# A decoder layer on one core: the search for an expert's threshold, two bits a round instead of one

## What is computed

```python
logits = xf @ router_w + router_b          # 4096 tokens x 8 experts
scores = softmax(logits, axis=-1)
G, idx = top_k(scores.T, 512)              # each expert takes its 512 best tokens
toks = xf[idx]
h1 = relu(toks @ w1 + b1)
eo = h1 @ w2 + b2
y = zeros_like(xf).at[idx].add(eo * G[..., None])
```

## Time and profile before

| | us |
|---|---|
| median of 3 runs | 1249.55 |
| lowest, highest run | 1247.36, 1250.38 |
| the profiled execution | 1243.2 |
| its span | 1241.5 |
| of it the 30 rounds, 972.87 to 1009.74 | 36.87 |
| TensorE busy in the span | 1125.6 |
| VectorE busy in the span | 971.6 |
| ScalarE busy in the span | 711.8 |

### The profile page before, as it was taken

How to read it: one execution, slowest core, us unless ns; L and a number is a source line. 1 busy time by engine, 2 the same in 40 slices (tenths; PEclk the granted TensorE clock), 3 DMA queues, 4 the chain that set the end, 5 groups by cost and what they waited for, 6 DMA issues and landing times. The chain is left out here.

```text
span 1241.5 us, 21939 instructions
## 1 busy us (share of the span) xinstructions
PE 1125.6 (91%) x7644; PEld 668.3 (54%) x7647; DVE 971.6 (78%) x2640; ACT 711.8 (57%) x1429; POOL 584.9 (47%) x676
## 2 busy tenths in 40 slices
PE   4599999999999999999999999999998229999997
PEld 2355555555555555444455454544334117988896
DVE  7688888888889789888888898988872677666653
ACT  6035555555455656777767777776674104566553
POOL 5666586765868563535353535350221004354524
PEclk9779999999999999999999999999999558999999
DMA  5551542525426345252525252424101604544413
GB/s 176 119 119 30 128 95 78 120 57 116 107 83 146 95 107 127 77 109 80 121 69 121 69 120 69 103 71 101 35 18 52 192 0 157 134 112 111 112 27 34
DMA packets 89328, 117.91 MB, mean 95 GB/s; under 512 B 12065, under 2 KB 59105, under 8 KB 89090
## 3 DMA queue, kind: packets, MB, share of 16 engines
q1 hardware_dynamic: 83074, 107.97, 33.9%
q0 software_dynamic: 6144, 8.52, 4.2%
HBM read 48.63 MB, written 16.91 MB: 53 GB/s over the span
## 5 line engine op out<-in xcount | busy, mean ns | idle before, releaser
L823 ACT ACTIVATE probs<-ps_st 128x512 f32<-128x512 f32 (+3 forms) x1024 | 476.6, 518 | 249.8 <-PE ps_st L647 245.4
L667 PE MATMUL ps_p<-kst,qst 63*128 63x512 f32 (+3 forms) x1024 | 371.4, 428 | 14.9 <-DVE mx L940 13.5
L938 DVE TENSOR_REDUCE mx<-ps_p 128x1 f32<-128x512 f32 x512 | 325.4, 681 | 58.6 <-PE ps_p L667 57.8
L647 PE MATMUL ps_st<-qst,kst 64*128 64x512 f32 (+3 forms) x1024 | 362.5, 420 | 9.5 <-ACT probs L823 8.5
L647 PEld LDWEIGHTS ps_st<-qst,kst 64*128 64x128 f32 x1024 | 166.3, 186 | 264.1 <-ACT probs L823 216.4
L940 DVE CUSTOM_DVE_ANT_0 ps_p<-ps_p,tri 128x128 f32<-128x128 f32 (+3 forms) x512 | 239.3, 513 | 16.4 <-PE ps_p L667 14.6
L628 PE MATMUL ps_o<-probs,vals 128*32 128x512 f32 (+3 forms) x2048 | 232.7, 527 | 0.0
L667 PEld LDWEIGHTS ps_p<-kst,qst 63*128 63x128 f32 x1024 | 169.1, 186 | 29.1 <-DVE mx L940 21.5
L468 POOL TENSOR_SCALAR lnw<-mv 128x4 f32<-128x4 f32 x24 | 5.0, 210 | 282.9 <-DVE mv L917 282.8
L533 POOL TENSOR_SCALAR_AFFINE_SELECT probs<-probs 128x512 f32<-128x512 f32 x128 | 79.6, 637 | 102.5 <-ACT probs L823 102.5
L1251 POOL DMA_INDIRECT out_dram<-moe_part,moe_ids x32 | 58.7, 1835 | 75.4 <-DVE moe_part L1614 69.0
(11 more groups left out here) (237 smaller groups left out, 1928.5 us busy)
## 6 DMA issues: line engine op xcount, KB each, us to landing
qst<-qk_h SPq DMA_DIRECT2D x64, 256.0 KB, 4.7
kst<-qk_h SPq DMA_DIRECT2D x64, 256.0 KB, 5.0
qst<-qk_l SPq DMA_DIRECT2D x32, 256.0 KB, 5.4
kst<-qk_l SPq DMA_DIRECT2D x32, 256.0 KB, 5.1
moe_w1r<-in_w_dram SPq DMA_DIRECT2D x8, 1024.0 KB, 5.1
moe_w2r<-in_w_dram SPq DMA_DIRECT2D x8, 1024.0 KB, 9.1
xin<-in_x_dram SPq DMA_DIRECT2D x8, 512.0 KB, 3.8
xres<-in_x_dram SPq DMA_DIRECT2D x8, 512.0 KB, 4.0
```

What stands on the lines that cost most here:

```text
L647: last = nc.tensor.matmul(out, kst[rows, t % 2, pair, kt * P:(kt + 1) * P], qst[rows, t % 2, pair, lo:S], start=True, stop=not masked)
L667: last = nc.tensor.matmul(ps_p1[:, i % 3, 0:keys], qst[rows, t % 2, pair, qt * P:(qt + 1) * P], kst[rows, t % 2, pair, 0:keys], start=True ...
L823: nc.scalar.activation(probs[:, kt, j, 0:n], ps_st[:, i % 2, 0:n], ACT.Exp, scale=float(DH) ** -0.5).then_inc(exp_done, 1)
L938: nc.vector.tensor_reduce(mx[:, g % 2, at:at + 1], bank, AX.X, ALU.max).then_inc(max_done, 1)
```

## The change

Each round now settles two bits and tries three candidates. VectorE counts the scores against two of them (`cand` columns 2 and 3) by two instructions, and ScalarE counts them against the third (column 1) by the function Sign of candidate minus score, summed. TensorE turns the sum of signs into a count by two accumulating products (`same` with a constant column, `same_half` with the signs), and sums the two counts by a third product with two columns. The number of candidates that are met, 0 to 3, is the value of the two bits: VectorE compares three sums with 512 and accumulates (`met`, `won`), and one instruction makes all the next candidates.

The candidates are kept as floats that hold integers, so the 30 bits are searched in two parts: the scores' patterns shifted right by 14 as floats (`high`) in 8 rounds, then the low 14 bits (put into `score`, with the difference of the high parts times 4^7 added) in 7 rounds. The candidates lie half below an integer, so that no sign is zero. In ScalarE's stream the 15 counts stand ahead of `high_w` of expert 0; VectorE waits for GpSimd's `consts` ahead of the search.

```diff
-        BITS = 30
+        HIGH, LOW, HALF = 8, 7, 0.5
...
-            for k in range(BITS):
+            pe.wait_ge(same_ready, 1)
+            for k in range(HIGH + LOW):
+                if k > 0:
+                    pe.wait_ge(cand_ready, k + 1)
+                nc.tensor.matmul(ps_h[:, 0, 0:1], same[:, :], half_all[:, :], start=True, stop=False)
+                pe.wait_ge(cnt_signs, k + 1)
+                nc.tensor.matmul(ps_h[:, 0, 0:1], same_half[:, :], cnt_sign[:, :], start=False, stop=True)
                 pe.wait_ge(cnt_ready, k + 1)
-                nc.tensor.matmul(ps_h[:, 0, 0:1], same[:, :], cnt[:, :], start=True, stop=True).then_inc(cnt_sum, 1)
+                nc.tensor.matmul(ps_h[:, 0, 1:3], same[:, :], cnt[:, :], start=True, stop=True).then_inc(cnt_sum, 1)
...
+            for k in range(HIGH + LOW):
+                act.wait_ge(cand_ready, k + 1)
+                    nc.scalar.activation(sign[:, :, :], high[:, :, :] if k < HIGH else score[:, :, :], ACT.Sign, bias=cand[:, 1:2], scale=-1.0,
+                                         accum_out=cnt_sign[:, :]).then_inc(cnt_signs, 1)
...
-            nc.vector.tensor_copy(same[:, :].rearrange("p (t e) -> p t e", e=E_N), own_row[:, :].unsqueeze(1).to_broadcast([P, P // E_N, E_N]))
+            link(nc.vector.tensor_copy(same[:, :].rearrange("p (t e) -> p t e", e=E_N), own_row[:, :].unsqueeze(1).to_broadcast([P, P // E_N, E_N])))
+            nc.vector.memset(half_all[:, :], float(NT * P // 2 // (P // E_N)))
+            nc.vector.tensor_scalar(out=same_half[:, :], in0=same[:, :], scalar1=-HALF, scalar2=None, op0=ALU.mult).then_inc(same_ready, 1)
...
-            nc.vector.memset(cand[:, :], 1 << (BITS - 1))
+            dve.wait_ge(consts, 1)
+            link(nc.vector.tensor_copy(steps[:, :], iota[:, 0:4]))
             dve.wait_ge(score_turned, 1)
             link(nc.vector.tensor_copy(score[:, :, :], ps_a[:, 0, 0:2 * P].rearrange("p (h k) -> p h k", h=2)))
-            for k in range(BITS):
-                bit = 1 << (BITS - 1 - k)
+            link(nc.vector.tensor_scalar(out=bits[:, :, :], in0=score[:, :, :].bitcast(I32), scalar1=2 * LOW, scalar2=None,
+                                         op0=ALU.arith_shift_right))
+            link(nc.vector.tensor_copy(high[:, :, :], bits[:, :, :]))
+
+            def round_of(k, values, left):
+                    for j in range(2):
+                        last = nc.vector.tensor_scalar(out=ge[:, j, :, :], in0=values[:, :, :], scalar1=cand[:, j + 2:j + 3], scalar2=0.0,
+                                                       op0=ALU.is_ge, op1=ALU.add, accum_out=cnt[:, j:j + 1])
+                last.then_inc(cnt_ready, 1)
...
+                    link(nc.vector.scalar_tensor_tensor(out=follow[:, :], in0=steps[:, :], scalar=float(4 ** (left - 1)),
+                                                        in1=cand[:, 0:1].to_broadcast([P, 4]), op0=ALU.mult, op1=ALU.add))
...
                 dve.wait_ge(cnt_sum, k + 1)
+                link(nc.vector.tensor_scalar(out=met[:, :], in0=ps_h[:, 0, 0:3], scalar1=float(CAP), scalar2=0.0,
+                                             op0=ALU.is_ge, op1=ALU.add, accum_out=won[:, :]))
+                return nc.vector.scalar_tensor_tensor(out=cand[:, :], in0=won[:, 0:1].to_broadcast([P, 4]), scalar=float(4 ** left),
+                                                      in1=follow[:, :], op0=ALU.mult, op1=ALU.add)
...
+            link(nc.vector.tensor_scalar(out=bits[:, :, :], in0=score[:, :, :].bitcast(I32), scalar1=4 ** LOW - 1, scalar2=None,
+                                         op0=ALU.bitwise_and))
+            nc.vector.tensor_copy(low[:, :, :], bits[:, :, :])
+            link(nc.vector.tensor_scalar(out=high[:, :, :], in0=high[:, :, :], scalar1=cand[:, 0:1], scalar2=float(4 ** LOW),
+                                         op0=ALU.subtract, op1=ALU.mult))
+            link(nc.vector.tensor_tensor(out=score[:, :, :], in0=high[:, :, :], in1=low[:, :, :], op=ALU.add))
+            nc.vector.tensor_scalar(out=cand[:, :], in0=steps[:, :], scalar1=float(4 ** (LOW - 1)), scalar2=-HALF,
+                                    op0=ALU.mult, op1=ALU.add).then_inc(cand_ready, 1)
+            dve.wait_ge(cand_ready, HIGH + 1)
```

More of the change, by code:

```diff
@@ L1090, in mixture @@
         score = sb("score", [P, 2, P], F32)
[L1091 to L1095, removed]
+        ge = sb("ge", [P, 2, 2, P], BF16)
+        bits = sb("bits", [P, 2, P], I32)
+        high = sb("high", [P, 2, P], F32)
+        low = sb("low", [P, 2, P], F32)
+        steps = sb("steps", [P, 4], F32)
+        cand = sb("cand", [P, 4], F32)
+        follow = sb("follow", [P, 4], F32)
+        met = sb("met", [P, 3], F32)
+        won = sb("won", [P, 1], F32)
+        cnt = sb("cnt", [P, 2], BF16)
+        cnt_sign = sb("cnt_sign", [P, 1], BF16)
+        sign = sb("sign", [P, 2, P], BF16)
+        same_half = sb("same_half", [P, P], BF16)
+        half_all = sb("half_all", [P, 1], BF16)
         above = sb("above", [P, 2, P], F32)
@@ L1151, in mixture @@
         cnt_ready = sem("cnt_ready")
+        cnt_signs = sem("cnt_signs")
+        cand_ready = sem("cand_ready")
+        same_ready = sem("same_ready")
         cnt_sum = sem("cnt_sum")
@@ L1403, in _ @@
             nc.scalar.activation(logits[:, :, :], logits[:, :, :], ACT.Exp).then_inc(exp_out, 1)
+            for k in range(HIGH + LOW):
+                act.wait_ge(cand_ready, k + 1)
+                with nc.allow_low_precision("sums of 256 signs are even and exact"):
+                    nc.scalar.activation(sign[:, :, :], high[:, :, :] if k < HIGH else score[:, :, :], ACT.Sign, bias=cand[:, 1:2], scale=-1.0,
+                                         accum_out=cnt_sign[:, :]).then_inc(cnt_signs, 1)
             def high_w(e, part):
@@ L1470, in _ @@
-                dve.wait_ge(cnt_sum, k + 1)
[L1471 to L1474, removed]
+                    for j in range(2):
+                        last = nc.vector.tensor_scalar(out=ge[:, j, :, :], in0=values[:, :, :], scalar1=cand[:, j + 2:j + 3], scalar2=0.0,
+                                                       op0=ALU.is_ge, op1=ALU.add, accum_out=cnt[:, j:j + 1])
@@ new lines, in round_of @@
+                last.then_inc(cnt_ready, 1)
+                if left > 0:
+                    link(nc.vector.scalar_tensor_tensor(out=follow[:, :], in0=steps[:, :], scalar=float(4 ** (left - 1)),
+                                                        in1=cand[:, 0:1].to_broadcast([P, 4]), op0=ALU.mult, op1=ALU.add))
+                else:
+                    link(nc.vector.tensor_scalar(out=follow[:, :], in0=cand[:, 0:1].to_broadcast([P, 4]), scalar1=HALF, scalar2=None, op0=ALU.add))
+                dve.wait_ge(cnt_sum, k + 1)
@@ new lines, in round_of @@
+                link(nc.vector.tensor_scalar(out=met[:, :], in0=ps_h[:, 0, 0:3], scalar1=float(CAP), scalar2=0.0,
+                                             op0=ALU.is_ge, op1=ALU.add, accum_out=won[:, :]))
+                return nc.vector.scalar_tensor_tensor(out=cand[:, :], in0=won[:, 0:1].to_broadcast([P, 4]), scalar=float(4 ** left),
+                                                      in1=follow[:, :], op0=ALU.mult, op1=ALU.add)
+            nc.vector.tensor_scalar(out=cand[:, :], in0=steps[:, :], scalar1=float(4 ** (HIGH - 1)), scalar2=-HALF,
+                                    op0=ALU.mult, op1=ALU.add).then_inc(cand_ready, 1)
@@ new lines, in _ @@
+            dve.wait_ge(cand_ready, 1)
+            for k in range(HIGH):
+                last = round_of(k, high, HIGH - 1 - k)
+                if k < HIGH - 1:
+                    last.then_inc(cand_ready, 1)
+                    dve.wait_ge(cand_ready, k + 2)
+                else:
+                    link(last)
+            link(nc.vector.tensor_scalar(out=bits[:, :, :], in0=score[:, :, :].bitcast(I32), scalar1=4 ** LOW - 1, scalar2=None,
+                                         op0=ALU.bitwise_and))
@@ L1475, in _ @@
+            dve.wait_ge(cand_ready, HIGH + 1)
+            for k in range(LOW):
+                last = round_of(HIGH + k, score, LOW - 1 - k)
+                if k < LOW - 1:
+                    last.then_inc(cand_ready, 1)
+                    dve.wait_ge(cand_ready, HIGH + k + 2)
+                else:
+                    link(last)
+            limit = cand[:, 0:1]
             with nc.allow_low_precision("counts up to 128 are exact"):
```

## The result

The changed kernel took 1236.6 us in the median of 4 runs (1234.6 to 1239.75), beside 1248.63 for the kernel before: a ratio of 0.992 with a 95% interval of 0.9897 to 0.9942, or 7.2 to 12.9 us less. The prediction was 1241.8 with a gain of 7.8; the direction is right and the gain too small. 1.3 us of what it missed lie in the search, by one term of the round; the rest is the spread of runs and the median that it started from.

What follows compares the result with a forecast made beforehand. The routing's search, a closed chain of 30 rounds in 36.87 us, was taken to bound what follows; 36.87 - 26.4 (15 rounds of 1.76) - 2.65 once-only = 7.8 saved, 1249.55 to 1241.8 us, range 1236.5 to 1247.5.

Steps and rivals of the forecast that it cites:

- the accumulated comparison: Each round, after the last product: comparison of three columns with accumulator and its read, 0.33 us against 0.20 before.
- the once-only terms: Work added once around the search, outside the rounds: 2.65 us in sum, 0.8 more with slow figures.
- (1): Ahead of the softmax's sum: a link, a memset and a 128x128 product delay the scores by 0.3 us (0.2 to 0.45).
- (2): Between score and first count: linked shift, conversion to float and first candidates add 0.85 us, or 1.1 if slow.
- (3): Between the search's two parts: mask, conversion, difference, sum and candidates add 1.5 us, or 1.9 with slow figures.
- (4): Ahead of the search: VectorE's wait for GpSimd's constants costs nothing; 0.6 us if GpSimd were 1 us later.
- (a): In each round ScalarE's sum comes last, so 3.0 us less is saved: 1244.8 us; chance 0.12.
- the forecast's own limit of 0.85: In each round, ScalarE's sign sum stays hidden if there by about 0.85 us; forecast at 0.71, slack 0.14.
- (b): ScalarE's Sign needs another function table, delaying only the first round: 1243.1 us, or an estimated 1244.5; chance 0.06.
- (c): At the experts, TensorE's clock meets the shifted work a step later: 1243.9 us; chance 0.06.
- (d): In the search ScalarE reloads a table every round, 15 us more: 1257 us; chance 0.04.
- (e): VectorE's counts do not overlap and linked steps take upper values, round 1.88 us: 1244.4 us; chance 0.06.

Runs made afterwards that it cites:

- the run with one wait less: Changed kernel with all three counts on VectorE, and TensorE's wait for the new candidates left out; one run took 1246.29 us.
- the version with the shorter search: Changed kernel with helper matrices, score shift and low-bit preparation taken off the path, difference and sum made one instruction; 1236.99 us, ratio to before 0.9905.

## Why the prediction was right, and where it was too small

**Right in mechanism.** The forecast reads 1 or 2 tenths for TensorE in the valley, where the row has 2 in both slices; nothing hangs on it. The valley of the earlier trace rows is bound by the search; the two counts are 0.41 apart (forecast 0.40); the last product is released by VectorE; ScalarE's weight rounding moved behind its last count (to 1005.06) at no cost, with the first remainder at 1024.85, 9.1 earlier than before when counted from `own_row`; what lies behind the flags took as long as before.

**The term that was mis-sized.** The round was forecast at 1.76 and took 1.66, outside the forecast's own bounds of 1.69 to 1.80. The step of the forecast that was mis-sized is the accumulated comparison: 0.33 to the new candidate in the forecast, 0.20 to 0.21 in the trace. Both of its parts were too large. The read was put at 0.14 after the start, by a line through 256 and 128 elements, and came at 0.09 (982.66 to 982.75); the line does not hold down to 3 elements. And the wait behind the read was taken from L1482, 0.10, where 0.03 was measured (982.83 to 982.86). L1482 stands behind two waits, for `consts` and for its own chain, and a second wait costs 0.06, as the run with one wait less showed on TensorE. That L1482's 0.10 is made of 0.04 and 0.06 is an inference; no run isolates it on VectorE. The traces agree with it in one place: the instruction that takes the scores from PSUM waits for the transposes alone in the kernel before and starts 0.72 to 0.73 after their start (three profiles); in the changed kernel and its variants it waits for VectorE's own last instruction too and starts at 0.79 to 0.80 (seven profiles). 15 rounds x 0.10 are 1.5 us more of gain than forecast; the once-only terms take 0.2 of them back.

**The once-only terms.** (1) ahead of the softmax's sum: forecast 0.3, measured 0.44 (`own_row` to the copy of the scores 2.61 before, 3.05 after). Of this 0.18 is the link and the two instructions, less than the 0.3; 0.20 is a longer multiplication, L1489, which was not foreseen (below); the last 0.06 is the later copy behind the transposes. (2) between the copy and the first count: forecast 0.85, measured 0.87 (1.33 against 0.46). (3) between the parts: 1.5, measured 1.58. (4) the wait for `consts`: nothing, as said. So the sum was 36.87 - 26.4 - 2.65 = 7.8 and would have been 36.87 - 24.9 - 2.9 = 9.1.

**The rivals.** (a) ScalarE's sum last: no. The activation took 0.51 and its accumulator's read 0.19, close to the values taken (0.51 and 0.2). But the read began 0.42 after the activation's start (981.40 to 981.82), not behind its end, so the sum was there at 0.61 where the forecast had 0.71. By the forecast's own limit of 0.85 that is a slack of 0.24 instead of 0.14; the run with Sign twice showed 0.28. That the sum is hidden was right, and its price was a choice between two bounds 0.4 apart, so luck had a part in it. (b) another table: no.

```profile
L794 ACT ACT_TABLE_LOAD x1 | 1.3, 1283 | 2.4 <-PEq L1735 2.4
```

That is the only load in the trace of the changed kernel, at the start as in the earlier trace rows; Sign ran with the table of Exp. By the Trainium skill (ScalarE: Activation LUTs, "What ACT_TABLE_LOAD costs") a switch would have been some 2.66 us; no run here switched. (c) the clock: busy time around the start of the experts, of the changed kernel's profile, whose first expert matmul began at 1028.96:

```profile
1029.00:1033.00 4.00, 4.00 (x12) 3.16 (x12) 2.68 (x3) 1.10 (x2) 2.06 (x2) 0.63 0.39 97
1033.00:1034.00 1.00, 1.00 (x5) 0.64 (x4) 0.74 (x2) 0.77 (x3) 0.00 (x0) 1.00 0.50 111
```

A mean of 0.63 over 4 us is 3.0 us at half (1.2 GHz) and 1.0 at full level, so the rise came 3.0 us after the first expert matmul instead of 4.2, and the stretch to the end was still 209.04. When the changed kernel ran again, the clock was at full level when the experts began:

```profile
1028.78:1033.00 4.22, 4.15 (x17) 3.15 (x18) 3.91 (x5) 2.45 (x5) 2.04 (x2) 1.00 0.49 109
```

Its stretch to the end was 207.7, and so was that of the version with the shorter search. The other eight profiles have 208.9 to 209.8. So the clock's part is about 1.3 us, less than the 2.1 allowed. (d) no: the round got shorter than forecast, and there was no load in it. (e) no: the counts overlap, 0.41 apart.

**The median.** The forecast carried the saving to a median of three runs, and the range (1236.5 to 1247.5) held the result by 0.1 us, which is luck: the same kernel measured again gave 1239.89. With 9.1 in place of 7.8 it would have said 1240.5, and from the median of four runs, 1248.63, 1239.5. The rest down to 1236.6 is the spread of runs. (The terms named for the high end add up to 1246.7 or 1247.7, not 1247.5.)

## What to carry to other kernels

A search that every engine waits for is a chain of latencies: take it link by link and ask what a wider round adds to the chain and what it adds beside it. Two bits a round paid only because another engine took the third count into its idle time; on one engine alone the wider round gave 7.2 of the 9.1 us back. Price the small instructions of a chain from rows of the same size and with the same number of waits, not along a line through large ones, and take the once-only work that such a change brings off the path, into waits that are there anyway.

## What the runs showed of the hardware that was not expected

A second semaphore wait in front of an instruction of TensorE cost 0.06 to 0.07 us, though the first had long been satisfied (0.20 against 0.14 in a round, 0.95 us over the 14 rounds).

VectorE and GpSimd slowed each other by which came first. A 128x256 product of two SBUF tensors took 0.42 us and GpSimd's select of 32x128 beside it 0.68 when VectorE's began first (the three profiles of the kernel before and of its 22 rounds, and the version with the shorter search). In the changed kernel it began 0.04 after the select and took 0.62 to 0.64, the select 0.53, in all six profiles of kernels with that order:

```profile
976.91 0.53 POOL L1242 TENSOR_SCALAR_AFFINE_SELECT moe_spread<-moe_spread 32x128 f32<-32x128 f32 x1
976.95 0.62 DVE L1489 TENSOR_TENSOR logits<-logits,moe_tot 128x256 f32<-128x256 f32 x1
```

The Trainium skill (SBUF — State Buffer, "Terms") states that the two engines share a port pair with an exclusive lock that is held for the full instruction. The order effect agrees with a shared resource; a full block doesn't fit, since VectorE's instruction ended at 977.57, only 0.13 after the select's end, and took 0.42 where it began first. (The profile's spans of GpSimd are rough, so the 0.13 is too.)

Activations with an accumulator follow one another every 0.49 to 0.51 us on ScalarE (984.00, 984.51 and 985.00 in the run with three bits), without one after 0.41 (981.92 and 982.34, second Sign in the run with Sign twice).

The stretch from the flags to the experts was 22.7 to 22.8 in five profiles and 24.0 to 24.2 in the other five. In four of these (changed kernel again, third count on VectorE, Sign twice, the version with the shorter search) VectorE's copy of the second expert's ids waited 2.9 us instead of 1.1, released by something that the profile calls remote. In the fifth (the run with one wait) that copy waited 1.1, and TensorE waited 1.78 for gathered rows instead of 0.39 in the changed kernel. What this is stays open.
